# Four last tiles instead of five by one-hot matmuls, base sums behind the last gatings, three weight conversions out of the routing

## The reference

```
x = x + tanh(g_xattn) * (softmax((LN(x) Wq' + bq)(ctx Wk')' / sqrt(128)) (ctx Wv' + bv)) Wo' + bo
p = softmax(LN(x) gate_w')                 # 8 experts
top 2 experts of each token, with weights p
x = x + tanh(g_ffn) * sum over the two:  p_k * (gelu(LN(x) w1[e]' + b1[e]) w2[e]' + b2[e])
```

## Time and profile before

| | |
|---|---|
| median of 3 runs | 93.9 us (93.62 to 93.94) |
| profiled execution | 94.14 us, of which the span is 92.4 us |
| busy | PE 77.5 us (84%), DVE 67.1 (73%), ACT 57.1 (62%), POOL 50.7 (55%) |
| chain that ended last | PE 60%, DVE 21%, ACT 5%, DMA 4%, issue 4%, POOL 3% |
| DMA | 12.58 MB, mean 136 GB/s |

### The profile page before, as it was taken

How to read it: one execution, slowest core, us unless ns; L and a number is a source line. 1 busy time by engine, 2 the same in 40 slices (tenths; PEclk the granted TensorE clock), 3 DMA queues, 4 the chain that set the end, 5 groups by cost and what they waited for, 6 DMA issues and landing times.

```text
span 92.4 us, 2742 instructions
## 1 busy us (share of the span) xinstructions
PE 77.5 (84%) x828; PEld 68.0 (74%) x828; DVE 67.1 (73%) x309; ACT 57.1 (62%) x174; POOL 50.7 (55%) x81
## 2 busy tenths in 40 slices
PE   4958898776957538999989999999999999899930
PEld 1355566465754434999989999999999999799920
DVE  2179728998969899999976777569788566538860
ACT  4284589998996595516557887577567657244000
POOL 6975498008777677872000089777877784026400
PEclk9999999996555555559999999999999999999999
DMA  1999999890111112551364534511111021393016
GB/s 19 316 395 369 418 433 426 257 286 29 58 32 61 58 58 71 161 149 34 86 138 110 107 89 115 143 48 44 59 39 32 25 62 32 49 289 123 0 48 179
DMA packets 11630, 12.58 MB, mean 136 GB/s; under 512 B 1363, under 2 KB 10599, under 8 KB 11360
## 3 DMA queue, kind: packets, MB, share of 16 engines
q1 hardware_dynamic: 9840, 9.74, 33.4%
q0 software_dynamic: 1088, 2.05, 6.9%
q10 hardware_dynamic: 688, 0.61, 2.3%
HBM read 8.18 MB, written 4.42 MB: 136 GB/s over the span
## 4 chain that ended last, share of the span: by engine, by line
PE 60%; DVE 21%; ACT 5%; DMA 4%; issue 4%; POOL 3%; DVEq 0%; POOLq 0%
PE bank L825 24%; PE bank L807 6%; PE bank L808 6%; PE bank L809 6%; PE bank L839 5%; PE bank L752 4%; DMA x_sb<-in_x 4%; PE bank L791 2%; POOL rstd L410 2%; DVE x L958 2%; PE bank L700 2%; DVE xn L894 2%; PE bank L821 2%; DVE stats L965 2%; DVE stats L901 1%
## 5 line engine op out<-in xcount | busy, mean ns | idle before, releaser
L607 ACT ACTIVATE hid<-bank,wp 128x128 f32<-128x128 f32 x92 | 26.4, 367 | 17.2 <-PE bank L809 17.2
L457 POOL DMA_INDIRECT results<-y_sb,in_rows x18 | 18.5, 1029 | 16.2 <-ACT y_sb L566 10.9
L825 PE MATMUL bank<-w_sb,hid 128*128 (+1 forms) x184 | 26.4, 288 | 0.0
L825 PEld LDWEIGHTS bank<-w_sb,hid 128*128 128x128 f32 x184 | 23.2, 198 | 0.0
L373 POOL DMA_INDIRECT dispatched<-rows,slot x16 | 16.3, 1016 | 9.9 <-DVE slot L1027 6.2
L807 PE MATMUL bank<-xs_t,w_hi 128*128 128x128 f16 x76 | 13.8, 219 | 0.3 <-DVE xs_t L1134 0.3
L808 PE MATMUL bank<-xs_t,w_hi 128*128 128x128 f16 x76 | 13.8, 219 | 0.0
L809 PE MATMUL bank<-xs_t,w_lo 128*128 128x128 f16 x76 | 13.8, 219 | 0.0
L1134 DVE COPY xs_t<-bank 128x256 f16<-128x256 f16 x19 | 5.4, 291 | 8.6 <-PE bank L791 7.5
L807 PEld LDWEIGHTS bank<-xs_t,w_hi 128*128 (+1 forms) x76 | 7.4, 98 | 0.5 <-DVE xs_t L1134 0.4
L808 PEld LDWEIGHTS bank<-xs_t,w_hi 128*128 (+1 forms) x76 | 7.4, 98 | 0.0
(11 more groups left out here) (174 smaller groups left out, 170.0 us busy)
## 6 DMA issues: line engine op xcount, KB each, us to landing
w_sb<-in_w SPq DMA_DIRECT2D x2, 2048.0 KB, 11.3
in_rows<-dispatched SPq DMA_DIRECT2D x23, 65.0 KB, 2.0
results<-zeros SPq DMA_DIRECT2D x1, 1024.0 KB, 5.3
res<-results SPq DMA_DIRECT2D x4, 256.0 KB, 3.7
dispatched<-pad_rows SPq DMA_DIRECT2D x9, 65.0 KB, 2.6
ctx_sb<-in_ctx_t SPq DMA_DIRECT2D x1, 512.0 KB, 4.8
wp<-in_wpack ACTq DMA_DIRECT2D x1, 342.0 KB, 3.4
results<-y_sb,in_rows POOLq DMA_INDIRECT x18
```

Source lines behind the costliest of these rows:

```text
L457: pool.indirect_dma_start(results_dram, bass.IndirectOffsetOnAxis(ap=in_rows[:].bitcast(U32)[:, t, TARGET:TARGET + 1], axis=0), y_sb[:, t, ...
L607: mm = act.activation(hid[:, t % HIDS, b, :], hid_ps[h % len(hid_ps)][:, (b % HALVES) * P:(b % HALVES + 1) * P], ACT.Gelu_apprx_tanh, bias ...
L825: mm = pe.matmul(to, hid[:, t % HIDS, b, :], w2_sb[:, e, b * P:(b + 1) * P], start=False, stop=b == BLOCKS - 1)
```

## The change

`LAST` becomes 4, so tiles 0 to 18 are scattered and tiles 19 to 22 are summed by one-hot matmuls. VectorE's two base sums each move one iteration later: the first behind the gating of tile 21, the second behind that of tile 22. In `sum_last` the last tile is done half by half (first bank with both parts, then the second) and the others part by part as before. Of the four `W1_HIGH` one stays in the routing; the second is issued behind the first Gelu instruction (which only loads the table), the third and fourth behind the copies of the gathered rows of tiles 1 and 2. Group 2's `ROOT` moves behind its `COPY_X1_T` on ScalarE.

```diff
-LAST, ONE_HOTS = 5, 10
+LAST, ONE_HOTS = 4, 10
...
-    ROOT: [16.7, 22.1, 27.4, 32.9],
+    ROOT: [16.7, 22.1, 27.9, 32.9],
...
-    W1_HIGH: [14.9, 20.6, 22.5, 26.3],
+    W1_HIGH: [14.9],
...
             act.activation(gelu_first[:], tanhs[:], ACT.Gelu_apprx_tanh)
+            weights_hi(w1_hi, w1_sb, ld_w1, w1hi_ok, 1)
...
                 if t < EARLY:
                     copy_first(t)
+                if t in (1, 2):
+                    weights_hi(w1_hi, w1_sb, ld_w1, w1hi_ok, t + 1)
...
-                for c in range(2):
+                def part(c, h):
                     pe.wait_ge(y16_ok, 2 * i + c + 1)
+                    for j in range(HALF):
...
+                        mm = pe.matmul(to, at, y_16[:, i, c, :], start=i == 0 and j == 0 and c == 0, stop=i == LAST - 1 and j == HALF - 1 and c == 1)
+                    if i == LAST - 1 and c == 1:
+                        mm.then_inc(last_ps[h], 1)
+
+                if i < LAST - 1:
+                    for c in range(2):
+                        for h in range(2):
+                            part(c, h)
+                else:
                     for h in range(2):
...
+                        for c in range(2):
+                            part(c, h)
...
-                if t == N_TILES - 2:
+                if t == N_TILES - 1:
                     summed = [base_sum(DVE_CHUNKS[0])]
-                if t == N_TILES - 1:
+                if t == N_TILES:
                     summed.append(base_sum(DVE_CHUNKS[1]))
```

More of the change, by code:

```diff
@@ L832, in sum_last @@
                     pe.wait_ge(xs_ok, N_TILES - EARLY)
-                for c in range(2):
+                def part(c, h):
                     pe.wait_ge(y16_ok, 2 * i + c + 1)
-                    for h in range(2):
[L836 to L841, removed]
+                    for j in range(HALF):
+                        to = sum_ps[h][:, j * P:(j + 1) * P]
+                        at = whose[:, i, (h * HALF + j) * P:(h * HALF + j + 1) * P]
+                        mm = pe.matmul(to, at, y_16[:, i, c, :], start=i == 0 and j == 0 and c == 0, stop=i == LAST - 1 and j == HALF - 1 and c == 1)
[6 more added lines that the diff above has]
+                else:
+                    for h in range(2):
+                        for c in range(2):
+                            part(c, h)
             experts = [slice(e, e + 1) for e in range(EXPERTS)]
```

## The result

Over 19 executions of each, side by side, the changed kernel took a median of 93.62 us and the kernel before 94.26. The ratio is 0.9865, 95% interval 0.9827 to 0.9904, so some 1.27 us of 94.2 less; forecast was 1.25 less. Single executions of both kernels scatter by more than that, so a pair of profiles shows where time is spent, and the ratios show how much the change is worth. The profiled execution of the changed kernel took 93.46.

The account below looks back on a forecast made before the run. The prediction took a chain of waits as the bound: routing to about 36, TensorE from 37 to 79, then the tail. Routing 0.60, clock -0.15 and tail 0.80 sum to 1.25, forecasting 92.7 (range 91.9 to 93.5).

Parts of the forecast that it names:

- The routing, 0.60 and with the clock 0.45: Routing: moving high halves away removes VectorE's 0.60 wait for the logits; 0.15 comes off for the clock.
- the 0.15 taken off for the clock: TensorE's return to 2.4 GHz: halfway between moving with the work (nothing lost) and staying at 41.7 (0.30 lost).
- rival A: TensorE's clock return stays where it is, so the routing gives 0.30; time 92.8, chance 0.24.
- rival E: TensorE's clock returns earlier and half of that is gained; 2.6 earlier would give 91.4; chance 0.03.
- The tail, 0.80: End of the kernel: four last tiles and later base sums gain 0.80, bounds 0 and 1.48.
- the last chunk, for which GpSimd started at 84.91, lands at 86.79: Tail: result loads go out 1.88 later, so GpSimd's last chunk lands at 86.79; gain 0.88 by this path.
- The last gating "0.04 late, nothing": Tail: VectorE's first base sum ends by 85.32, so the last gating starts 0.04 late, costing nothing.
- rival D: Tail: the first base sum, waiting for its load, holds the last gating; 94.4 or more, chance 0.06.
- part 3: Tail: base sums behind the last gatings; the second is exposed, taking 0.7 to 1.27, ending between 86.7 and 87.6.
- The halves, nothing: Last tile's matmuls half by half: first half done after 24 not 28, 0.22 at most, but adds wait anyway: nothing.
- Rival B: Tail: later result loads leave VectorE's second and GpSimd's last sum as the end; tail 0.1, time 93.35, chance 0.13.
- Rival C: Routing: GpSimd's back-to-back sends and a late first row load hold back 0.2 or more; about 93.0, chance 0.09.

Follow-up runs that it names:

- the routing alone: Kernel before with only the high halves 1 to 3 moved and the root behind the copy of x1: ratio 0.9914 to the kernel before.
- plain order: Changed kernel with the last tile summed part by part like the others, not half by half: ratio 0.9877 to the kernel before.
- the sums early: Changed kernel with VectorE's two base sums ahead of the gatings of tiles 21 and 22, as before: ratio 0.9945 to the kernel before.
- five last tiles: Changed kernel with LAST = 5, base sums at their old places, tile 18 summed together with tile 19: ratios 0.9829 and 0.987 to the kernel before.
- the tail alone: Changed kernel with the routing's edits taken back: ratio 0.9975 to the kernel before.
- both longer programs: Changed kernel with TensorE's 9 opening matmuls replaced by 75 of 64 columns, or 84 of 56: ratios 0.987 and 0.9909 to the kernel before.
- the 75 opening matmuls: Changed kernel with 75 matmuls of 64 columns for TensorE's 9 of 512, 132 instructions more: ratio 0.987 to the kernel before.
- changed again: The changed kernel itself, unaltered, measured once more against the kernel before: ratio 0.988.

## Why the prediction was right, and which terms were not

The sum was right, 1.25 against 1.27 (0.78 over all executions), and two of its terms were off in opposite directions. That they made up for each other is luck.

*The routing, 0.60 and with the clock 0.45: measured 0.81, interval 0.5 to 1.1.* The steps came out to a few hundredths: the copy at 25.20, the logits' matmuls at 25.64, the choice at 26.91 without the 0.60 of idle time in front, the sends back to back, the first cast of loaded rows at 45.83. The first hidden matmul stood 0.73 earlier in the changed kernel and 0.53 in the routing alone. The 0.60 lies inside the interval; the 0.15 taken off for the clock is the weak step. Granted clock rows put the return to 2.4 GHz at 41.7 in the kernel before, but at 39.9, 39.5 and 39.1 in three profiles of the changed kernel and its plain order, at 40.6 with the routing alone, 40.7 with the sums early, 39.6 with five last tiles, and at 39.2 with the tail alone, whose routing is that of before. For the changed kernel, the routing alone and the tail alone (length, PE busy, clock, DMA share, GB/s):

```profile
39.50:40.00 0.50, 0.50 (x4) 0.60 0.70 175
```

```profile
40.50:41.00 0.50, 0.50 (x6) 0.85 0.37 125
```

```profile
39.00:39.50 0.50, 0.50 (x10) 0.84 0.51 157
```

So rival A, a return that stays at 41.7, is out, and its 0.30 lies below the measured interval. The Trainium skill (TensorE: Matmul & The Clock Gate, What's actually happening) says that the gate's window is free-running. A return that differs by 2.6 between executions agrees with that; the conclusion that the prediction drew from it, that the return stays, does not hold. The clock also makes the pair of profiles misleading: the changed kernel's last transposes stood 1.27 earlier, of which 0.73 was there at the first hidden matmul and the rest came with a clock that returned 1.8 sooner in that execution. Against the work that is 1.1 sooner, and half of it is about the 0.54 that is left, as rival E reckons; but the tail alone had an early return too, so the change is not shown to be its cause.

*The tail, 0.80: measured 0.23 by itself (interval 0.2 slower to 0.6 faster), or 0.46 as the change less the routing.* This is the term that was mis-sized, and the step in it is "the last chunk, for which GpSimd started at 84.91, lands at 86.79": the loads were moved by 1.88 and their landing was kept at 4.4. The issue did move as said (79.59 is 0.56 later, that is 1.83 less the 1.27). The landing was 5.8, 5.5, 4.8 and 5.9 in four of five profiles with 19 scattered tiles and TensorE's program unlengthened, and 3.7 to 4.5 in five with loads at the old place. At the old place the loads are done, or nearly, when the piece of the instruction queue begins; moved a tile later they took it in, in four of five profiles. The later place by itself is not the reason: there too the landing was 4.1 to 4.4 in the three profiles in which the piece held up no packet of the loads. The trace does not name the engine of a packet, but in the tail alone and in both longer programs the packet that comes late starts within 0.02 of the piece's end. That the piece delays what waits on its engine is shown by this. What it costs the mean time is not: in what share of executions it hits is not settled, and neither longer program was measurably faster than the changed kernel.

*The last gating "0.04 late, nothing"* held: it waits for TensorE only. The sums at their old places, 0.75 slower, are rival D's mechanism with its sign: a sum that waits for a load in front of a gating makes TensorE wait for it (1.55 in that profile). In part 3 the two instructions of a base sum without GpSimd beside them were put at some 0.7; the second sum in the changed kernel took 0.88, from 86.18 to 87.06.

*The halves, nothing,* held. *Rival B*, the results in TensorE's place, is what most profiles with 19 scattered tiles show. It was priced at a tail of 0.1 and given 0.13; with a measured tail of 0.2 to 0.5 the truth lies between it and the forecast. *Rival C* did not happen: the row loads were there. The 2.8 in its account is the longest landing of the 15 later row loads; of the first eight none took over 2.4 in the kernel before.

## What to carry to other kernels

When work moves from an engine to a round trip through HBM, forecast the landing from the place at which the transfer now stands, not from its old duration: look at what else is on the DMA engines then, down to the page's instruction queue. A wait for data of uncertain time belongs behind the last instruction that another engine needs. And where the clock's return differs from execution to execution, compare a stage's own length between profiles, not its place on the time axis.

## What the runs showed of the hardware

TensorE's program arrives in pieces of 16 KB while it runs, each a single packet of 0.9 to 1.8 us. That this queue carries TensorE's program is seen from the 75 opening matmuls: all seven pieces came earlier, the first at 14.2 instead of 20.1, while the first piece of the other instruction queue within the span (q14, 8 KB) stayed at 20.4 (20.3). The 132 more instructions moved the last piece by some 3 us, from 5.3 to 2.2 behind the start of tile 18's scatter. A transfer spread over all 16 engines is not done until the one with the piece has caught up: loads whose last packets end 4.8 to 5.6 behind their issue ended at 5.7 to 6.7, and a scatter's 2.2 to the next issue became 3.1 and 4.3. With one and the same program on TensorE the piece began at 2.9, 3.0, 3.1 (sums early, changed again, changed) and 5.2 (tail alone) behind the loads' issue, so its place can't be set to better than 2 us or so by counting instructions.

Two base sums side by side: VectorE's second instruction took 0.42 alone (changed kernel) and 0.91 beside GpSimd's sum (plain order), as the 0.83 in the rows of before had suggested.
